# A running sum over sorted edges: chunks of 2048 in place of steps of 1024, and the mask as bytes by a broadcasting transfer

## Chip, core and metric

One Trainium2 chip, one of its cores. The metric is the device time of one execution in microseconds (us). TensorE is called PE, VectorE DVE, ScalarE ACT, GpSimd POOL and SyncE SP, as in the profile. SP issues nearly all plain transfers, POOL the indirect ones.

## What is computed

Two graph layers on 12,500 nodes of 64 channels and 212,500 edges, which come sorted by their target `dst`. Cut to what matters here (the second layer):

```python
h = relu(layernorm(x))
e = concatenate([h[src], edge_attr], axis=1)        # 212500 x 128
e = e @ W1a + b1a                                   # 212500 x 128
e = relu(batchnorm(e) * g1a + be1a)                 # statistics over all edges
# ( @ W2a + b2a ) and the sum over the edges of a node change places in the kernel
s = segment_sum(e, dst, 12500)                      # 12500 x 128
x = x + mlp(concatenate([h, s @ W2a + degree * b2a]))
```

The first layer is an edge network too, with a maximum over the edges of a node in place of the sum.

## The kernel before

It runs six stages one after the other, each a block in which every engine has its own program and waits on semaphores. A barrier of all engines ends a stage.

1. Index work: where each node's edges begin and end in the sorted list, and a mask that is 1 where an edge has the same target as the edge before it. It lies in `m01` (104 rows of 2048 edges, bf16) and goes to DRAM as `same_sum`. SP fills `recv_edges` with 1 MB transfers (L348), POOL scatters into it.
2. The edge network of layer 1: POOL gathers rows of source nodes.
3. Maxima are collected per node, the layer norm follows.
4. The hidden layer of layer 2, in 416 blocks of 512 edges: POOL gathers, PE transposes and multiplies, `finish` (L1126) writes hidden values into `hid` and takes their statistics; SP's `store` (L994) writes two blocks at a time, 512 KB, to `hid_edges`, channels on partitions.
5. The running-sum stage (L1150 to L1257), which nearly the whole change is about.
6. Node sums are taken as differences, then the node network.

Stage 5 walks over 212,992 edges (padded) in 208 steps k of STEP = 1024 edges. Channels lie on the 128 partitions, edges along the free dimension. A running sum is restarted at each new target by multiplying it by the mask: total[e] = mask[e] * total[e-1] + relu(gain * hid[e] + shift). The sum at the last edge of a node is that node's sum. In a step:

- SP `load` (L1176) fetches 1024 columns of `hid_edges`, 4 KB for each partition, into one of U = 8 slots (free again after the relu), then the step's mask, 2 KB on one partition, into one of R = 4 slots.
- PE `spread` (L1207) multiplies a column of ones by the mask row, so that the mask stands on all partitions in PSUM (`ps_mask`).
- ACT `relu` (L1228) writes `act_out`, two slots; it waits for the scan of step k-2.
- DVE `running_sum` (L1248) scans: `total` from `ps_mask`, `act_out` and the last column of the previous step's `total`.
- PE `turn_back` (L1215) transposes the 1024 columns with eight 128x128 transposes, so that edges lie on partitions, into `ps_back`.
- ACT `rows_out` (L1234) copies them to `rows`, SP `store` (L1188) writes them back, 512 KB, over the space of `hid_edges` that the step has read.
- SP `confirm` (L1183) waits for a store to land and raises `steps_out`; POOL (L1195) gathers the last row of each node's edges, 128 nodes at a time (100 gathers), once `steps_out` has reached the number in `steps_needed`.

The order on an engine is written by `pipeline(eng, steps, unroll, stages)` (L78 and on): at turn i each stage of the list, in the order of the list, is run for step i minus its lag. So ACT runs relu(k), rows_out(k-1), relu(k+1), rows_out(k), and SP runs load(k), store(k-5), confirm(k-8).

Of the kernel before, what the change touches and what calls it, by code (L numbers as in the profile page):

```python
# [20 lines left out]
P = 128  # L21
# [6 lines left out]
I16 = mybir.dt.int16  # L28

# [49 lines left out]
def pipeline(eng, steps, unroll, stages):  # L79
# [9 lines left out]
    assert rounds * unroll == steps and rounds > first and last <= unroll  # L89
# [14 lines left out]
    for step in range(steps - unroll, steps + last):  # L104
        peeled(step)


def gnn_kernel(nc, x, src, dst, edge_attr, W1, b1, W2, b2, W1a, b1a, g1a, be1a, W2a, b2a,
# [7 lines left out]
    STEP = 2 * BLK  # L116
    CO = 2048
# [5 lines left out]
    STEP_BITS = STEP.bit_length() - 1  # L123
    assert STEP == 1 << STEP_BITS
# [23 lines left out]
    def dram(name, shape, dt=F32):  # L148
        return nc.dram_tensor(name, shape, dt, kind="Internal").ap()
# [3 lines left out]
    same_sum = dram("same_sum", (EP,), BF16)  # L153
# [5 lines left out]
    hid_edges = dram("hid_edges", (NBLK // 2, P, 2 * BLK))  # L159
# [4 lines left out]
    with stack:  # L164
# [25 lines left out]
        steps_needed = tensor(stack, "steps_needed", [1, NI], I32)  # L190
# [51 lines left out]
        with ExitStack() as s1:  # L242
# [5 lines left out]
            mbig = tensor(s1, "mbig", [NCO, CO], BF16)  # L248
            firsts = tensor(s1, "firsts", [NCO, CO // GRP])
# [71 lines left out]
            def _(sp):  # L321
# [32 lines left out]
                sp.wait_ge(masks_made, 2)  # L354
                sp.dma_start(same_sum.rearrange("(p c) -> p c", c=CO), m01[:, :]).then_inc(masks_out, 16)
# [168 lines left out]
            def _(dve):  # L524
# [73 lines left out]
                nc.vector.tensor_scalar(mbig[:, :], m01[:, :], 2 * BIG, -BIG, ALU.mult, ALU.add).then_inc(masks_made, 1)  # L598

# [39 lines left out]
                once.link(nc.vector.tensor_scalar(column_end_i[:, :], column_end_i[:, :], STEP_BITS, None, ALU.logical_shift_right))  # L639
                once.link(nc.vector.tensor_scalar(steps_needed[:, :], column_end_i[:, :], 1, None, ALU.add))  # L640
# [290 lines left out]
        with ExitStack() as s4:  # L931
# [6 lines left out]
            hid = tensor(s4, "hid", [P, U // 2, 2, BLK])  # L938
# [22 lines left out]
            stored = [sem(f"stored4_{i}") for i in range(U // 2)]  # L961
# [7 lines left out]
            def _(sp):  # L969
# [24 lines left out]
                def store(r, s):  # L994
                    if s % 2 == 0:
                        return
                    at_least(sp, hid_made, r * U + s + 1)
                    sp.dma_start(hid_v[:, bass.ds(r * (U // 2) + s // 2, 1), :].rearrange("p a f -> p (a f)"),
                                 hid[:, s // 2, :, :].rearrange("p b q -> p (b q)")).then_inc(stored[s // 2], 16)

                pipeline(sp, NBLK, U, [(0, load), (5, store)])
                for q in range(U // 2):
                    sp.wait_ge(stored[q], 16 * (NBLK // U))
# [121 lines left out]
            def _(dve):  # L1125
                def finish(r, s):  # L1126
                    k = r * U + s
                    at_least(dve, multiplied, k + 1)
                    at_least(dve, stored[s // 2], 16 * r)
                    part = hid[:, s // 2, s % 2, :]  # L1130
# [19 lines left out]
        with ExitStack() as s5:  # L1150
            U = 8
            R = 4
            JS = STEP // P
            STEPS = EP // STEP
            hid = tensor(s5, "hid5", [P, U, STEP])
            mask_in = tensor(s5, "mask_in5", [1, R, STEP], BF16)
            ones5 = tensor(s5, "ones5", [1, P], BF16)
            act_out = tensor(s5, "act_out", [P, 2, STEP])
            total = tensor(s5, "total", [P, 2, STEP])
            rows = tensor(s5, "rows5", [P, R, JS * HID])  # L1160
            ps_mask = [banks(s5, f"ps_mask5_{b}", [P, STEP]) for b in range(2)]
            ps_back = [banks(s5, f"ps_back5_{b}", [P, JS * HID]) for b in range(2)]
            loaded = [sem(f"loaded5_{i}") for i in range(U)]
            stored = [sem(f"stored5_{i}") for i in range(R)]
            begun, mask_spread, relu_done, sum_done, back_turned, rows_made = (
                sem(n + "5") for n in ("begun", "mask_spread", "relu_done", "sum_done", "back_turned", "rows_made"))
            steps_out, sums_got, pool_passed = sem("steps_out"), sem("sums_got"), sem("pool_passed5")
# [274 lines left out]
```

## Time and profile before

| | us |
|---|---|
| median of 3 runs | 6878.51 |
| lowest and highest | 6867.25, 6896.64 |
| span of the profiled execution, first to last instruction | 5487.3 |
| median less span | 1391.2 |
| PE busy | 2916.4 (53%) |
| DVE busy | 2048.7 (37%) |
| ACT busy | 1440.8 (26%) |
| POOL busy | 3571.2 (65%) |

The profile holds one execution. Its own time beyond the span isn't recorded; what a timed run has besides the span is taken from the median. Times in the trace count from the span's start. Busy time counts work on data, not waits, branches or the issuing of transfers. The page cuts the span in 40 slices of 137 us and shows the busy share of an engine in tenths; the row PEclk has the granted TensorE clock in tenths of 2.4 GHz. Where an engine stood idle, the trace names what ended the idle time ("releaser").

### The profile page before, as it was taken

What the parts mean: (1) busy time and instruction counts of PE and PEld (TensorE: products, weight loads), DVE (VectorE), ACT (ScalarE), POOL (GpSimd) and SP (SyncE); (2) the same over time, 40 slices, a digit from 0 to 9 for tenths busy, and PEclk for the clock granted to TensorE, in tenths of its full rate; (3) what the DMA queues carried; (4) which work ended last, traced back from release to release, by engine and by line L of the source; (5) the groups of instructions that cost most, each with busy time, mean ns of one, the idle gap of its engine ahead of it and who ended that gap; (6) DMA issues with size and microseconds to landing.
All of it is one profiled execution on the core that took longest, in us unless ns stands there. A gap on an engine that the chain in (4) does not pass through costs nothing. (4 is left out here: it accounts for less than half of the span.)

```text
span 5487.3 us, 47739 instructions
## 1 busy us (share of the span) xinstructions
PE 2916.4 (53%) x8675; PEld 1611.3 (29%) x8675; DVE 2048.7 (37%) x2739; ACT 1440.8 (26%) x2694; POOL 3571.2 (65%) x3776
## 2 busy tenths in 40 slices
PE   2035555555555555521555555555555554888887
PEld 2023222332332233210222222222222222455455
DVE  7123333333333333344222222222222223666774
ACT  8011111111111111111222222222222221666663
POOL 6677777777777777766777777777777776111112
PEclk9975555556555655555666666666666666555556
DMA  9623233233233322322333333333333333899992
GB/s 353 207 62 78 78 80 80 77 79 80 78 78 80 80 76 80 80 53 64 105 103 106 107 101 106 107 104 103 107 105 103 107 107 89 311 322 321 321 322 70
DMA packets 396210, 695.12 MB, mean 127 GB/s; under 512 B 138632, under 2 KB 195730, under 8 KB 389410
## 3 DMA queue, kind: packets, MB, share of 16 engines
q1 hardware_dynamic: 250135, 558.29, 29.3%
q0 software_dynamic: 119328, 128.91, 12.4%
q10 hardware_dynamic: 26706, 7.50, 0.6%
q14 instruction: 31, 0.25, 0.0%
q8 instruction: 10, 0.16, 0.0%
HBM read 349.70 MB, written 344.74 MB: 127 GB/s over the span
## 5 line engine op out<-in xcount | busy, mean ns | idle before, releaser
L1014 POOL DMA_INDIRECT pairs<-norm_table,send_idx x1664 | 1573.9, 946 | 526.1 <-issue 506.8
L729 POOL DMA_INDIRECT send_in<-send_table,send_idx x1664 | 1574.3, 946 | 507.7 <-issue 505.1
L1028 PE MATMUL ps_pairs<-ident,pairs 128*128 128x128 f32 x1664 | 400.3, 387 | 991.1 <-issue 744.3
L1131 DVE TENSOR_SCALAR hid<-ps_hid,vec 128x512 f32<-128x512 f32 x416 | 312.2, 751 | 1384.0 <-PE ps_hid L1035 1384.0
L1035 PE MATMUL ps_hid<-pairs_t,w1a 128*128 128x512 f32 x832 | 711.2, 953 | 0.0
L1028 PEld LDWEIGHTS ps_pairs<-ident,pairs 128*128 128x128 f32 x1664 | 262.2, 195 | 1438.9 <-issue 1279.9
L1070 ACT COPY pairs_t<-ps_pairs 128x512 f32<-128x512 f32 x416 | 244.0, 586 | 1473.6 <-PE ps_pairs L1028 1473.6
L741 PE MATMUL ps_msg<-hidden,w_twice 128*128 128x512 f32 x416 | 431.1, 1140 | 307.9 <-ACT hidden L794 307.9
L763 PE MATMUL ps_send<-ident,send_in 128*128 128x128 f32 x832 | 216.3, 410 | 689.7 <-DMA send_in<-send_table,send_idx 689.7
L1254 DVE TENSOR_TENSOR_SCAN total<-ps_mask,total,act_out 128x1024 f32<-128x1024 f32 x208 | 488.8, 2350 | 215.3 <-ACT act_out L1232 215.1
L1201 POOL DMA_INDIRECT node_sums<-hid_edges,end_idx x100 | 94.6, 946 | 643.4 <-SPq L1186 636.9
L810 DVE TENSOR_TENSOR_SCAN maxima<-mask,maxima,ps_msg 128x512 f32<-128x512 f32 x208 | 266.2, 1280 | 600.3 <-PE ps_msg L741 600.3
L1220 PE MATMUL ps_back<-ident,total 128*128 128x128 f32 x1664 | 410.3, 427 | 98.1 <-DVE total L1254 98.1
L1220 PEld LDWEIGHTS ps_back<-ident,total 128*128 128x128 f32 x1664 | 327.2, 221 | 278.9 <-DVE total L1254 259.6
L819 DVE TENSOR_TENSOR_SCAN filled<-mask,filled,ps_recv 128x512 f32<-128x512 f32 x208 | 266.2, 1280 | 322.9 <-ACT mask L782 322.9
L763 PEld LDWEIGHTS ps_send<-ident,send_in 128*128 128x128 f32 x832 | 137.9, 203 | 781.4 <-DMA send_in<-send_table,send_idx 781.4
L782 ACT COPY mask<-ps_mask 128x512 f32<-128x512 f32 x208 | 121.9, 586 | 898.1 <-PE ps_mask L759 898.1
L794 ACT ACTIVATE hidden<-joined 128x512 f32<-128x512 f32 x208 | 130.9, 629 | 827.3 <-DVE joined L827 827.3
L827 DVE TENSOR_TENSOR joined<-filled,ps_send 128x512 f32<-128x512 f32 x208 | 143.1, 688 | 493.1 <-PE ps_send L763 493.1
L1134 DVE BATCH_NORM_STATS2 stats<-hid 128x512 f32 (+1 forms) x416 | 288.3, 693 | 98.1 <-DVE hid L1131 97.5
L756 PE MATMUL ps_recv<-ident,recv_in 128*128 128x128 f32 x832 | 210.8, 405 | 136.9 <-DMA mask_in<-same_max 136.9
L1238 ACT COPY rows<-ps_back 128x1024 f32<-128x1024 f32 x208 | 210.5, 1012 | 255.3 <-PE ps_back L1220 255.3
(176 smaller groups left out, 3184.6 us busy)
## 6 DMA issues: line engine op xcount, KB each, us to landing
hid_edges<-hid SPq DMA_DIRECT2D x208, 512.0 KB, 2.9
hid<-hid_edges SPq DMA_DIRECT2D x208, 512.0 KB
hid_edges<-rows SPq DMA_DIRECT2D x208, 512.0 KB, 3.8
recv_edges<-node_sums SPq DMA_DIRECT2D x52, 1024.0 KB
recv_in<-recv_edges SPq DMA_DIRECT2D x208, 256.0 KB
max_edges<-max_rows SPq DMA_DIRECT2D x208, 256.0 KB, 2.1
edge_in<-in_edge_attr_dram SPq DMA_DIRECT2D x415, 128.0 KB, 3.1
send_in<-send_table,send_idx POOLq DMA_INDIRECT x1664
```

Source lines behind the costliest of these rows:

```text
L729: pool.indirect_dma_start(out=send_in[:, s, j, t, :], out_offset=None, in_=send_table, in_offset=bass.IndirectOffsetOnAxis(ap=send_idx[:, ...
L741: nc.tensor.matmul(ps_msg[:, :], w2_twice[:, :], hidden[:, s % 2, :], start=True, stop=True).then_inc(msg_done, 1)
L763: mm = nc.tensor.transpose(ps_send[s % 2][:, j::J], send_in[:, s, j, :, :].rearrange("p t c -> p (t c)"), ident[:, :])
L810: nc.vector.tensor_tensor_scan(maxima[:, s % 2, :], mask[:, s % 2, :], ps_msg[:, :], maxima[:, 1 - s % 2, BLK - 1:BLK], ALU.min, ALU.max). ...
L819: nc.vector.tensor_tensor_scan(filled[:, s % 2, :], mask[:, s % 2, :], ps_recv[s % 2][:, :], filled[:, 1 - s % 2, BLK - 1:BLK], ALU.min, A ...
L1014: pool.indirect_dma_start(out=pairs[:, s, j, 0:C], out_offset=None, in_=norm_table, in_offset=bass.IndirectOffsetOnAxis(ap=send_idx[:, s / ...
L1028: mm = nc.tensor.transpose(ps_pairs[s % 2][:, j::J], pairs[:, s, j, :], ident[:, :])
L1035: nc.tensor.matmul(ps_hid[s % 2][:, :], w1a[:, :], pairs_t[:, s % 2, :], start=True, stop=True).then_inc(multiplied, 1)
L1131: nc.vector.tensor_scalar(part, ps_hid[s % 2][:, :], vec[:, 0:1], None, ALU.add).then_inc(hid_made, 1)
L1134: nc.vector.bn_stats(stats[:, bass.ds(k, 1), :].rearrange("p a q -> p (a q)"), part[:, 0:valid]).then_inc(stats_made, 1)
L1220: mm = nc.tensor.transpose(ps_back[s % 2][:, j * P:(j + 1) * P], total[:, s % 2, j::JS], ident[:, :])
L1254: nc.vector.tensor_tensor_scan(total[:, s % 2, :], ps_mask[s % 2][:, :], act_out[:, s % 2, :], total[:, 1 - s % 2, STEP - 1:STEP], ALU.mul ...
```

## The change

- Stage 5 goes over 104 chunks of 2048 edges, 1 MB and 8 KB per partition for each load and each store. Relu and scan work in two halves of 1024, transposes in two groups of eight; the relu is written in place over `hid` (four slots), so that a slot comes free after the scan.
- The mask of a chunk is fetched from DRAM by a transfer that repeats its 2048 bytes for all 128 partitions, into one of two slots; it is of type uint8. The mask product on PE and its PSUM tiles are gone; all eight PSUM banks serve `ps_back`.
- The orders are new: SP runs store(k-5), load_mask(k-3), load(k), confirm(k-8); ACT relu and rows_out of the chunk before last, in halves by turns.
- Stage 4 stores four blocks (1 MB) at a time. Stage 1 makes a copy of the mask in bytes. `pipeline` takes a number of steps that the unrolling doesn't divide.

```diff
-    for step in range(steps - unroll, steps + last):
+    for step in range((rounds - 1) * unroll, steps + last):
...
-                sp.wait_ge(masks_made, 2)
-                sp.dma_start(same_sum.rearrange("(p c) -> p c", c=CO), m01[:, :]).then_inc(masks_out, 16)
+                sp.wait_ge(masks_made, 3)
+                sp.dma_start(same_sum.rearrange("(p c) -> p c", c=CO), m01_bytes[:, :]).then_inc(masks_out, 16)
...
+                nc.vector.tensor_copy(m01_bytes[:, :], m01[:, :]).then_inc(masks_made, 1)
...
-                    if s % 2 == 0:
+                    if s % 4 != 3:
                         return
                     at_least(sp, hid_made, r * U + s + 1)
...
             @block.sync
                 def load(r, s):
                     k = r * U + s
-                    at_least(sp, relu_done, k - U + 1)
-                    sp.dma_start(hid[:, s, :], hid_v[:, bass.ds(k, 1), :].rearrange("p a f -> p (a f)")).then_inc(loaded[s], 16)
-                    at_least(sp, mask_spread, k - R + 1)
-                    sp.dma_start(mask_in[:, s % R, :], mask_v[:, bass.ds(k, 1), :].rearrange("t a c -> t (a c)")).then_inc(loaded[s], 16)
+                    at_least(sp, sum_done, 2 * (k - HR + 1))
+                    sp.dma_start(hid[:, s % HR, :], hid_v[:, bass.ds(k, 1), :].rearrange("p a f -> p (a f)")).then_inc(loaded[s % HR], 16)
+
+                def load_mask(r, s):
+                    k = r * U + s
+                    at_least_apart(sp, sum_done, 2 * (k - 1), sp_passed)
+                    sp.dma_start(masks[:, s % 2, :], mask_v[bass.ds(k, 1), :].rearrange("k c -> (k c)").partition_broadcast(P)).then_inc(masks_in[s % 2], 16)
...
                 def store(r, s):
                     k = r * U + s
-                    at_least(sp, rows_made, k + 1)
+                    at_least(sp, rows_made, 2 * (k + 1))
...
-                pipeline(sp, STEPS, U, [(0, load), (5, store), (U, confirm)])
+                pipeline(sp, CHUNKS, U, [(5, store), (3, load_mask), (0, load), (8, confirm)])
...
             @block.tensor
+                def turn_back(r, s, h):
+                    k = r * U + s
+                    if h == 0:
+                        at_least(pe, sum_done, 2 * (k + 1))
+                    at_least(pe, rows_made, 2 * k + h - 3)
+                    for j in range(JS // 2):
+                        mm = nc.tensor.transpose(ps_back[s % 2 * 2 + h][:, j * P:(j + 1) * P], total[:, s % 2, h * (JS // 2) + j::JS], ident[:, :])
+                    mm.then_inc(back_turned, 1)
...
             @block.scalar
+                def relu(r, s, h):
+                    if h == 0:
+                        at_least(act, loaded[s % HR], 16 * (r * (U // HR) + s // HR + 1))
+                    part = hid[:, s % HR, h * HALF:(h + 1) * HALF]
+                    nc.scalar.activation(part, part, ACT.Relu, bias=shift[:, 0:1], scale=gain[:, 0:1]).then_inc(relu_done, 1)
+
+                def rows_out(r, s, h):
+                    k = r * U + s
+                    at_least(act, back_turned, 2 * k + h + 1)
+                    if h == 0:
+                        at_least(act, stored[s % R], 16 * (r * (U // R) + s // R))
+                    nc.scalar.copy(rows[:, s % R, h * HALF:(h + 1) * HALF], ps_back[s % 2 * 2 + h][:, :]).then_inc(rows_made, 1)
+
+                pipeline(act, CHUNKS, U, [(0, lambda r, s: relu(r, s, 0)), (2, lambda r, s: rows_out(r, s, 0)),
+                                          (0, lambda r, s: relu(r, s, 1)), (2, lambda r, s: rows_out(r, s, 1))])
...
             @block.vector
+                def running_sum(r, s, h):
+                    k = r * U + s
+                    if h == 0:
+                        at_least(dve, masks_in[s % 2], 16 * (r * (U // 2) + s // 2 + 1))
+                    at_least(dve, relu_done, 2 * k + h + 1)
+                    if h == 0:
+                        at_least(dve, back_turned, 2 * (k - 1))
+                    at_least(dve, sum_done, 2 * k + h)
+                    before = total[:, 1 - s % 2, CHUNK - 1:CHUNK] if h == 0 else total[:, s % 2, HALF - 1:HALF]
+                    part = slice(h * HALF, (h + 1) * HALF)
+                    nc.vector.tensor_tensor_scan(total[:, s % 2, part], masks[:, s % 2, part], hid[:, s % HR, part],
+                                                 before, ALU.mult, ALU.add).then_inc(sum_done, 1)
```

## Rows read from the trace of the kernel before

**Rows 1.** The page, 40 slices of the span: PE, its clock, DMA.
```profile
PE   2035555555555555521555555555555554888887
PEclk9975555556555655555666666666666666555556
DMA  9623233233233322322333333333333333899992
```

**Rows 2.** Table by stretches, stage 5: length, busy us of each engine, clock, DMA share, GB/s.
```profile
4700.00:5360.00 660.00, 568.55 (x1961) 332.96 (x1960) 460.78 (x197) 421.63 (x394) 88.00 (x93) 0.50 0.93 321
```

**Rows 3.** Groups, 4700 to 5360 us: line, out<-in, shapes, count, busy us, mean ns, idle before.
```profile
L1254 DVE TENSOR_TENSOR_SCAN total<-ps_mask,total,act_out 128x1024 f32<-128x1024 f32 x197 | 462.9, 2350 | 200.8 <-ACT act_out L1232 200.8
L1220 PE MATMUL ps_back<-ident,total 128*128 128x128 f32 x1568 | 386.6, 427 | 91.4 <-DVE total L1254 91.4
L1212 PE MATMUL ps_mask<-mask_in,ones 1*128 1x512 bf16 x393 | 202.5, 616 | 0.0
```

**Rows 4.** Waits, 4700 to 5360 us: who waited for whom, us, times, longest.
```profile
DVE total L1254 <- ACT act_out L1232: 200.8, 197, 1.7
```

**Rows 5.** Timeline from 4998 us: start, duration, engine, line, operation, idle before it.
```profile
4997.76 2.35 DVE L1254 TENSOR_TENSOR_SCAN total<-ps_mask,total,act_out 128x1024 f32<-128x1024 f32 x1 [0.44 <-ACT act_out L1232]
...
5000.24 1.97 PE L1220 MATMUL ps_back<-ident,total 128*128 128x128 f32 x8
...
5002.24 1.01 ACT L1238 COPY rows<-ps_back 128x1024 f32<-128x1024 f32 x1 [0.63 <-PE ps_back L1220]
5003.15 1.24 ACT L1232 ACTIVATE act_out<-hid,shift,gain 128x1024 f32<-128x1024 f32 x1
5003.28 0.35 SPq L1191 DMA_DIRECT2D hid_edges<-rows  x1
...
5004.48 2.35 DVE L1254 TENSOR_TENSOR_SCAN total<-ps_mask,total,act_out 128x1024 f32<-128x1024 f32 x1 [0.43 <-ACT act_out L1232]
```

**Rows 6.** SP's queue: packets, MB, engine share; 4700-5360, 4668-4671, 30-60 us.
```profile
q1 hardware_dynamic: 56839, 205.92, 90.1%
q1 hardware_dynamic: 270, 0.97, 90.2%
q1 hardware_dynamic: 1548, 10.61, 84.4%
```

**Rows 7.** Tile hid_edges, 4700 to 5360 us: the stores of 512 KB, issue to landing.
```profile
DMA to landing us min/median/max: 2.9/3.9/4.9
```

**Rows 8.** Tile hid_edges, 2600 to 4500 us (stage 4): the same.
```profile
DMA to landing us min/median/max: 2.7/2.9/3.1
```

**Rows 9.** Timeline, the start of stage 5.
```profile
4666.00 0.34 SPq L1179 DMA_DIRECT2D hid<-hid_edges  x1
...
4666.40 0.28 SPq L1181 DMA_DIRECT2D mask_in<-same_sum  x1
...
4670.50 2.49 ACT L1232 ACTIVATE act_out<-hid,shift,gain 128x1024 f32<-128x1024 f32 x2 [6.46 <-DMA mask_in<-same_sum]
...
4671.88 4.84 DVE L1254 TENSOR_TENSOR_SCAN total<-ps_mask,total,act_out 128x1024 f32<-128x1024 f32 x2 [5.58 <-ACT act_out L1232]
```

**Rows 10.** Timeline, the end of stage 5: last scan, last gather.
```profile
5367.97 2.35 DVE L1254 TENSOR_TENSOR_SCAN total<-ps_mask,total,act_out 128x1024 f32<-128x1024 f32 x1 [0.52 <-ACT act_out L1232]
...
5379.33 0.94 POOL L1201 DMA_INDIRECT node_sums<-hid_edges,end_idx  x1 [0.30 <-issue]
```

**Rows 11.** Timeline, the end of stage 4: SP's last two stores, and bn_aggr.
```profile
4641.09 11.15 SPq L998 DMA_DIRECT2D hid_edges<-hid  x2
...
4652.13 11.42 DVE L232 BATCH_NORM_AGGREGATE sums<-stats 128x2 f32<-128x2496 f32 x1
```

**Rows 12.** Stage 1: DVE's mask instruction (timeline), POOL's wait for the fills.
```profile
158.49 0.68 DVE L598 TENSOR_SCALAR mbig<-m 104x2048 bf16<-104x2048 bf16 x1
...
POOL recv_edges L406 <- SPq L347: 16.0, 2, 15.7
```

More of the change, by code:

```diff
@@ L88, in pipeline @@
     first = 2 if last else 1
-    assert rounds * unroll == steps and rounds > first and last <= unroll
+    assert rounds > first and last <= unroll
     def peeled(step):
@@ L116, in gnn_kernel @@
     STEP = 2 * BLK
+    CHUNK_BITS = (4 * BLK).bit_length() - 1
+    assert 4 * BLK == 1 << CHUNK_BITS
     CO = 2048
@@ L960, in gnn_kernel @@
             gathered = [sem(f"gathered4_{i}") for i in range(U)]
-            stored = [sem(f"stored4_{i}") for i in range(U // 2)]
+            stored = [sem(f"stored4_{i}") for i in range(U // 4)]
             idx_copied, w_in, turned, copied, multiplied, hid_made, stats_made, root_ready, root_made = (
@@ L1128, in finish @@
                     at_least(dve, multiplied, k + 1)
-                    at_least(dve, stored[s // 2], 16 * r)
-                    part = hid[:, s // 2, s % 2, :]
+                    at_least(dve, stored[s // 4], 16 * r)
+                    part = hid[:, s // 4, s % 4, :]
                     nc.vector.tensor_scalar(part, ps_hid[s % 2][:, :], vec[:, 0:1], None, ALU.add).then_inc(hid_made, 1)
@@ L1221, in turn_back @@
                     mm.then_inc(back_turned, 1)
-                pe.wait_ge(begun, 2)
-                pipeline(pe, STEPS, U, [(0, spread), (1, turn_back)])
+                pipeline(pe, CHUNKS, U, [(0, lambda r, s: turn_back(r, s, 0)), (0, lambda r, s: turn_back(r, s, 1))])
             @block.scalar
             def _(act):
-                def relu(r, s):
-                    k = r * U + s
-                    at_least(act, loaded[s], 32 * (r + 1))
-                    at_least(act, sum_done, k - 1)
-                    nc.scalar.activation(act_out[:, s % 2, :], hid[:, s, :], ACT.Relu, bias=shift[:, 0:1], scale=gain[:, 0:1]).then_inc(relu_done, 1)
@@ L1234, in rows_out @@
-                def rows_out(r, s):
-                    k = r * U + s
-                    at_least(act, back_turned, k + 1)
-                    at_least(act, stored[s % R], 16 * (r * (U // R) + s // R))
-                    nc.scalar.copy(rows[:, s % R, :], ps_back[s % 2][:, :]).then_inc(rows_made, 1)
-                pipeline(act, STEPS, U, [(0, relu), (1, rows_out)])
+                def relu(r, s, h):
[3 more added lines that the diff above has]
+                    nc.scalar.activation(part, part, ACT.Relu, bias=shift[:, 0:1], scale=gain[:, 0:1]).then_inc(relu_done, 1)
```

88 lines of the change are left out of this document (35 added, 53 removed).

## The prediction

> **What bounds the kernel now.** I read the page first, then one table by stretches, then the groups, the waits and a timeline of the running-sum stage (the fifth stage), because nearly every edit is in it. The page's DMA row is at 9 in the slices of this stage (the 35th to the 39th) and at 2 or 3 in the long gather stages before it, and the clock row falls to 5 [rows 1]. PE's own row stands at 5 in those gather stages, with the clock at 5 or 6. So the first suspicion is that the stage is bound by transfers. The stretch 4700 to 5360 us confirms DMA 93% busy at 321 GB/s, but also PE 569 of 660 us at a granted clock of 0.50, the 1.2 GHz level [rows 2]. In the groups no engine is full: DVE's scan takes 2350 ns x 197 and still idles 200.8 us, the transposes make 386.6 us and the mask product 202.5 us of PE's time [rows 3]. What ends DVE's idle time is always ACT's relu, never a DMA [rows 4].
>
> The timeline shows why. From the end of a scan (4997.76 + 2.35 = 5000.11): transposes 5000.24 to 5002.21, copy 5002.24 to 5003.25, relu to 5004.39, next scan of the same parity 5004.48 [rows 5]. ACT does relu(k+1) only behind rows_out(k-1), which waits for the transposes of sum k-1. That loop takes 6.72 us for two steps of 1024 edges. Its links follow each other without a gap, so the stage is bound by a handshake of engines, with DMA close behind. In 2048-edge units the period is 6.7 us, and I compare all that follows with it.
>
> **The change, part by part.** Write T for the time of a 2048-edge chunk afterwards, s(m) for the end of its second half scan.
>
> Removed: the mask product (197 of 2x512 columns in the stretch, 202.5 us of PE) and the order relu behind rows_out of the previous step. Relu now needs only its load. So the old loop is gone. Engine work per chunk: DVE 2 x 2.35 plus a handshake, about 4.9 us; ACT two relus of 1.24 and two copies of 1.01, 4.5; PE 16 transposes, 3.8 at 1.2 GHz [rows 5]. None of these reaches 6.7.
>
> DMA per chunk: 1.05 MB in, 1.05 MB out, and new 262 KB for the mask written to 128 partitions, where 4 KB went before. Rates, each divided by the queue's share of the engines: 346 GB/s in this stage (205.92 MB, 660 us, 90.1%), 358 at its start where only loads run (0.97 MB, 3 us), 419 for the 1 MB fills of 8 KB per partition (10.61 MB, 30 us, 84.4%) [rows 6]. No row has loads with 8 KB rows. So 1 MB out takes 2.5 us, 1 MB in 2.5 to 2.9, the mask 0.6 (by the fill's rate) to 1.0 (small rows; no transfer of 128 rows from one 2 KB source appears), the gathers 0.2. Sum 5.8 to 6.8 with a middle of 6.2: by DMA alone the stage would be between 13% shorter and unchanged.
>
> Added: a wait that decides, in SP's order. In a step SP does store(m-2), load_mask(m), load(m+3). store(m-2) waits for both row halves of chunk m-2, and the mask DMA sits behind that wait and then, on the same queue, behind the 1 MB just issued. Yet sum m cannot start without that mask. This is a new loop over two chunks:
> - from s(m-2) to the store's issue: 0.13 + transposes 1.97 + 0.04 + copy 1.01 + relu of the second half 1.24 + copy 1.01, less two overlaps of 0.1, is 5.2 us [rows 5]. The second eight transposes end by 3.9 and are hidden by copy and relu.
> - from the store's issue to the mask's landing: a 512 KB store lands 3.9 us after issue in this stage [rows 7] and 2.9 in the uncrowded stage before [rows 8]. With 1.25 us of that being bytes (at 419 GB/s), 1.65 is fixed. A 1 MB store: 1.65 + 2.5 = 4.15; the mask behind it adds 0.6 to 1.0: 4.9. Upper end: with the 1.0 us of crowding that 3.9 shows, and bytes at 346 GB/s, 6.5. Lower end 4.5. I take 5.5.
> - the two half scans: two scans in a row took 4.84 us at the start of the stage [rows 9], with the handshake to the mask 4.9. A scan with both operands in SBUF and byte masks has no row; I take the PSUM one, with -0.2 to +0.3 us each as bounds.
> The sum is 15.6. PE is busy half the time instead of 86%; the gather stages with that share show a clock of 5 or 6 [rows 1], so a part of the transposes may run at 2.4 GHz, where 1.97 becomes 1.0: less 0.2. That makes 15.4 for two chunks, T = 7.7 us against 6.7. DMA then has 1.5 us of slack per chunk and engines more: the loop sets the pace.
>
> That a transfer does wait behind the one ahead of it is shown at the stage's start: load at 4666.00, its 2 KB mask issued at 4666.40, and relu starts at 4670.50 although relu needs both only; loading 512 KB at 358 GB/s is 1.5 us and the rest is latency and queueing [rows 9]. On order, the Trainium skill ("DMA: Bandwidth & Descriptors", Queues, rings and completion order) says that each DMA engine consumes descriptors of a ring in order, though a later one may finish first; this agrees with the start of the stage, and speaks for the loop. The same page (Rules for kernel authors) asks for 128 partitions and at least 1 MiB per DMA for the highest bandwidth; here the 1 MB fills do move more per busy time than the 512 KB transfers, so by that rule the stage would take the DMA sum's 6.2 instead of 7.7, which is the rival B1 below.
>
> Start: mask(0) is issued behind three 1 MB loads. The 4.5 us that the first 512 KB took, 2.5 MB more at 2.7 us, and 0.8 for the mask are 12.0 us to landing, so s(0) = 17.0 and s(1) = 21.8 (today the first scan starts after 5.9 us). Then 51 pairs: s(103) = 21.8 + 102 T = 807.2. Today the last scan ends 704.3 us after the stage's first load (5367.97 + 2.35 - 4666.00 [rows 9, 10]). Tail: today the last gather starts 9.0 us after the last scan. After: 4.9 to the last store, 4.2 to its landing, then four gathers that need chunk 103 at 1.25 apart: 13.1. Difference: 807.2 + 13.1 - 704.3 - 9.0 = 102 T - 678.4 = +107 us.
>
> Edits at nothing: the hidden-layer stage stores 1 MB every four blocks instead of 512 KB every two. It is paced by POOL's gathers, the same hid slots come free at least four blocks (20 us) ahead, and the last store, issued about 4652, lands around 4656 while bn_aggr alone runs 11.42 us from 4652.13 [rows 11]; without that cover it would cost 1.3 us. The mask copy to bytes in the first stage is one DVE instruction of about the 684 ns of its neighbour, at most 2; POOL's scatters, behind it, wait up to 15.7 us for the fills anyway [rows 12]. The semaphore rename and shift cost nothing.
>
> The profile gives 5487.3 us of span, the timed runs 6878.5; the 1391 us outside the span I take as constant. If they scaled with the span, +107 would be +134. Sum: 6878.5 + 107 = 6985.5, about 6985.
>
> **The rivals.**
> A (forecast): the mask loop, T from 7.2 to 8.3: +56 to +168.
> B1: the mask does not queue behind the store (or only its tail). Then the loop is 5.2 + 0.6 + 2.3 + 4.8 = 12.9, under 6.5 a chunk, and DMA sets 6.2 to 6.4: -46 to -26 us, say 6840. For it: fills at 419 GB/s. Against it: the stage start, and that all these transfers go through one queue.
> B2: the same with loads no faster than 358 and a mask of 1.0 us: T 6.6 to 6.9, -5 to +25, about 6888.
> C: slower still. 128 reads of the same 2 KB are not priced by bytes. From 1 us more on for the mask the loop reaches 16.6, T 8.3 and more, +168 to +230: 7046 to 7109. Nothing in the profile shows such a read; only its place in the loop speaks for it.
> D: the clock returns to 2.4 GHz for most of the stage: pair 14.6, T 7.3, +66. It stays inside A.
>
> **How the numbers follow.** A with D 0.66, B1 0.12, B2 0.12, C 0.10. A time within 0.5% (34 us) is about what a measurement can't tell from no change. B1 lies on that edge and beyond with part of it; A's lower end spills a little into "same". Faster 0.11, same 0.15, slower 0.74. The range leaves out most of B1 and the far end of C: 6885 to 7080, the likeliest case A holding 6934 to 7047.
>
> **What would show it.** Right: in the timeline of the stage DVE's first half scan waits 2 us or more for the mask's DMA, every time; the store is issued about 5.2 us behind s(m-2) and the mask's landing 5 to 6 us later; DMA share falls from 93% to about 80 to 88%; chunks are 7.7 apart. Wrong: DMA still at 93% or more with chunks under 6.7 apart (B1, B2), or the mask's landing over 7 us behind the store's issue (C). A first scan earlier than 9 us into the stage would refute the start's term, a wait for hid slots in the stage before the zero there.

## Result and profile after

| | before | after |
|---|---|---|
| median, us | 6877.78 (4 runs) | 7075.07 (4 runs) |
| lowest to highest | 6867.25 to 6896.64 | 7069.56 to 7079.55 |
| ratio, 95% interval | | 1.0283, 1.0266 to 1.0299 |

The changed kernel is slower by 197 us. The prediction said 6985 with a range of 6885 to 7080: the direction and the mechanism hold, the size does not. +107 was forecast, so the cost was taken at a little over half. 7075 is above the 7047 at which the likeliest case of the prediction ended. It lies in the range, by 5 us, only because the range's upper end had been drawn for rival C, whose cause is not the one found below. That much is luck.

One thing has to be said of the numbers first. The profiled execution of before spans 5487 us, and I took the 1391 us up to its timed runs for work outside the span. That is wrong. The trace of after spans 7068.9 us at a time of 7071, and a second trace of before 5473.9 at a time of 5476. The kernels ran on several chips. On one kind a stall comes at nearly every turn of the loops in the gather stages, on the other there is none. Before takes about 6880 us on the first kind (chip 13; for the first result no chip is noted) and 5477 on the second (chips 4, 9 and 10). That it is the chip, and not something else of the occasion, is likely but not shown. The difference between the two kernels is nearly the same on both kinds, and a chunk of after takes 8.58 and 8.61 us on them (below); before has been traced on the second kind only. So stage 5 can be read from any of these traces, and each ratio is taken to runs of before on the same chip. A difference in us between two changed kernels goes by way of before.

The page of after, answering to [rows 1]:

```profile
PE   1033333333333333331233333333333333333336
PEclk9975555555666555565565656565666566656666
DMA  9312221111221121221222222222222222677783
```

The slices are longer (177 us), and in stage 5, from the 35th on, DMA stands at 6 to 8 where it stood at 9. In numbers, for a stretch of stage 5 (answering to [rows 2]), then SP's queue in the same stretch ([rows 6]):

```profile
6200.00:6800.00 600.00, 232.01 (x1104) 208.74 (x1104) 327.03 (x140) 288.30 (x276) 113.67 (x65) 0.61 0.78 278
```

```profile
q1 hardware_dynamic: 29785, 162.58, 75.7%
```

DMA is busy 78% and moves 278 GB/s, against 93% and 321. PE is busy 39%, DVE 55%, ACT 48%: nothing is full. What DVE waits for, in the groups and the waits ([rows 3, 4]):

```profile
L1258 DVE TENSOR_TENSOR_SCAN total<-masks,total,hid 128x1024 f32<-128x1024 uint8 x140 | 329.1, 2351 | 279.8 <-DMA masks<-same_sum 272.5
L1220 PE MATMUL ps_back<-ident,total 128*128 128x128 f32 x1104 | 232.0, 396 | 371.9 <-DVE total L1258 371.9
```

```profile
DVE total L1258 <- DMA masks<-same_sum: 272.5, 70, 7.5
```

The scan's time is unchanged at 2351 ns, with bytes in SBUF as its mask. 272.5 of its 279.8 idle us end with the landing of a mask. The timeline of two chunks shows the loop (answering to [rows 5]; start, duration, engine, line):

```profile
6479.00 4.80 DVE L1258 TENSOR_TENSOR_SCAN total<-masks,total,hid 128x1024 f32<-128x1024 uint8 x2 [7.04 <-DMA masks<-same_sum]
...
6483.93 3.33 PE L1220 MATMUL ps_back<-ident,total 128*128 128x128 f32 x16 [8.98 <-DVE total L1258]
6483.98 0.33 SPq L1184 DMA_DIRECT2D hid<-hid_edges  x1
6484.62 4.81 DVE L1258 TENSOR_TENSOR_SCAN total<-masks,total,hid 128x1024 f32<-128x1024 uint8 x2 [0.82 <-DMA masks<-same_sum]
...
6486.02 1.01 ACT L1238 COPY rows<-ps_back 128x1024 f32<-128x1024 f32 x1 [8.54 <-PE ps_back L1220]
6486.93 1.24 ACT L1231 ACTIVATE hid<-hid,shift,gain 128x1024 f32<-128x1024 f32 x1
6488.07 1.00 ACT L1238 COPY rows<-ps_back 128x1024 f32<-128x1024 f32 x1
...
6489.10 0.36 SPq L1198 DMA_DIRECT2D hid_edges<-rows  x1
...
6489.70 0.33 SPq L1189 DMA_DIRECT2D masks<-same_sum  x1
6490.30 0.94 SPq L1184 DMA_DIRECT2D hid<-hid_edges  x1
...
6494.21 0.36 SPq L1198 DMA_DIRECT2D hid_edges<-rows  x1
6494.81 0.48 SPq L1189 DMA_DIRECT2D masks<-same_sum  x1
6496.16 4.81 DVE L1258 TENSOR_TENSOR_SCAN total<-masks,total,hid 128x1024 f32<-128x1024 uint8 x2 [6.73 <-DMA masks<-same_sum]
```

Scans end at 6483.80. Transposes, copy, relu and copy follow, and the store is issued at 6489.10, 5.30 us later. The mask is issued at 6489.70, and the scans that need it begin at 6496.16. The loop is 17.16 us for two chunks, 8.58 each. The chunks between, of the other parity, run the same loop with a lag of 5.6 us rather than half the period. So DVE's waits come by turns: 7.04 us at one chunk, 0.82 at the next. Over chunks 12 to 91 of this trace the means are: 5.1 us from the end of a sum to its store's issue, 7.5 from there to the scan that needs the mask (6.4 to 9.3), 4.8 for the two half scans.

Start and end of stage 5 (answering to [rows 9, 10]):

```profile
6050.18 2.42 SPq L1184 DMA_DIRECT2D hid<-hid_edges  x3
...
6052.64 0.44 SPq L1189 DMA_DIRECT2D masks<-same_sum  x1
...
6062.07 9.75 DVE L1258 TENSOR_TENSOR_SCAN total<-masks,total,hid 128x1024 f32<-128x1024 uint8 x4 [11.76 <-DMA masks<-same_sum]
```

```profile
6945.35 4.81 DVE L1258 TENSOR_TENSOR_SCAN total<-masks,total,hid 128x1024 f32<-128x1024 uint8 x2 [1.44 <-DMA masks<-same_sum]
```

```profile
6962.85 0.95 POOL L1208 DMA_INDIRECT node_sums<-hid_edges,end_idx  x1 [0.30 <-issue]
```

From the first load to the last gather's start the stage takes 912.7 us, and took 713.3 [rows 9, 10]. The 199 us between them are the whole difference of the kernels.

### The profile page after: what moved, and what is told of

The parts are those of the page before. It is cut to its first block and busy times, and to the rows that moved or that the text cites. A ratio compares the mean times of both kernels' runs of the same rounds, so it can differ in the third digit from the quotient of the medians.

```text
span 7068.9 us, 44176 instructions
## 1 busy us (share of the span) xinstructions
PE 2417.4 (34%) x8259; PEld 1492.4 (21%) x8259; DVE 2039.6 (29%) x2739; ACT 1421.3 (20%) x2694; POOL 3637.2 (51%) x3776
## 5 line engine op out<-in xcount | busy, mean ns | idle before, releaser
L1040 PE MATMUL ps_hid<-pairs_t,w1a 128*128 128x512 f32 x832 | 623.8, 842 | 1000.4 <-ACT pairs_t L1075 572.1
L1258 DVE TENSOR_TENSOR_SCAN total<-masks,total,hid 128x1024 f32<-128x1024 uint8 x208 | 489.0, 2351 | 410.9 <-DMA masks<-same_sum 399.9
L1033 PE MATMUL ps_pairs<-ident,pairs 128*128 128x128 f32 x1664 | 334.4, 337 | 692.4 <-ACT pairs L1081 493.6
L1208 POOL DMA_INDIRECT node_sums<-hid_edges,end_idx x100 | 163.6, 1636 | 773.7 <-SPq L1193 767.4
L1220 PE MATMUL ps_back<-ident,total 128*128 128x128 f32 x1664 | 346.2, 393 | 572.1 <-DVE total L1258 572.1
L746 PEld LDWEIGHTS ps_msg<-hidden,w_twice 128*128 128x128 f32 x416 | 99.7, 298 | 1906.4 <-ACT hidden L799 1522.9
L1220 PEld LDWEIGHTS ps_back<-ident,total 128*128 128x128 f32 x1664 | 310.2, 218 | 607.8 <-issue 324.3
L1040 PEld LDWEIGHTS ps_hid<-pairs_t,w1a 128*128 128x128 f32 x832 | 170.0, 254 | 1055.0 <-ACT pairs_t L1075 589.6
L1231 ACT ACTIVATE hid<-hid,shift,gain 128x1024 f32<-128x1024 f32 x208 | 258.6, 1244 | 7.5 <-DMA hid<-hid_edges 7.4
```

Source lines behind the costliest of these rows:

```text
L746: nc.tensor.matmul(ps_msg[:, :], w2_twice[:, :], hidden[:, s % 2, :], start=True, stop=True).then_inc(msg_done, 1)
L1033: mm = nc.tensor.transpose(ps_pairs[s % 2][:, j::J], pairs[:, s, j, :], ident[:, :])
L1040: nc.tensor.matmul(ps_hid[s % 2][:, :], w1a[:, :], pairs_t[:, s % 2, :], start=True, stop=True).then_inc(multiplied, 1)
L1220: mm = nc.tensor.transpose(ps_back[s % 2 * 2 + h][:, j * P:(j + 1) * P], total[:, s % 2, h * (JS // 2) + j::JS], ident[:, :])
L1231: nc.scalar.activation(part, part, ACT.Relu, bias=shift[:, 0:1], scale=gain[:, 0:1]).then_inc(relu_done, 1)
L1258: nc.vector.tensor_tensor_scan(total[:, s % 2, part], masks[:, s % 2, part], hid[:, s % HR, part], before, ALU.mult, ALU.add).then_inc(sum ...
```

## Experiments

"A chunk takes" means below: the time from the first half scan to the last (both in the row of the scan, the number after "x208" being the least, median and largest duration), less 2.4 us, over 103. By that after has 8.58 us and before 6.73 for 2048 edges.

**The two kernels on the other kind of chip.** `before_again` and `after_again` are the kernels unchanged.

> The kernel before, unchanged, for a second trace of it. The profiled execution of before spans 5487 us while its timed runs take 6878; the one of the changed kernel spans 7069 and its runs take 7075. If the 1391 us are stalls that one trace of before happened not to have, this trace spans about 6870, its gather stages (2 and 4) have a stall at each turn of their loops of 14 and 11 us, and its running-sum stage takes the same 714 us as in the first trace. If the 1391 us lie outside the span, it spans about 5487 again. If the running-sum stage has stalls of its own, it is longer than 714 here and the comparison by stage has to be made again.

> The changed kernel itself, unchanged, beside the kernel before on the chip of the experiments, where before takes 5477 us and not 6878. If the difference of the two kernels comes from the running-sum stage alone, it is +190 to +205 us here too (5667 to 5682), and the stage shows chunks 8.6 us apart. If the stalls of the loops on the first chip took part in the difference, it is smaller here, +107 or less.

Measured: before 5475.67 with a span of 5473.9, after 5678.17, ratio 1.0368 (1.0351 to 1.0386), so +202 here against +197. The line of POOL's waits for ACT in stage 2, of after (first kind of chip), then of before_again:

```profile
POOL send_in L734 <- ACT send_idx L781: 781.5, 54, 16.3
```

```profile
POOL send_in L729 <- ACT send_idx L776: 3.6, 11, 0.5
```

54 waits of about 14 us in a loop of 52 turns of four steps; the same wait comes to 3.6 us in all on the other kind, at most 0.5 at a time. What ACT stalls on at the turn no trace names. The queue that the profile calls q14 instruction moved 12 packets in stages 2 to 4 of after and 11 in those of before_again, so more fetching of code does not show. Loads and scans of stage 5, before_again, then after_again, with after_again's masks from issue to landing:

```profile
L1179 SPq DMA_DIRECT2D hid<-hid_edges x208: 327/333/1779, 4653.3 to 5341.6; - x104
```

```profile
L1184 SPq DMA_DIRECT2D hid<-hid_edges x104: 327/345/1043, 4655.5 to 5529.3; - x104
L1258 DVE TENSOR_TENSOR_SCAN total<-masks,total,hid x208: 2349/2350/2353, 4668.5 to 5557.9; 128x1024 f32<-128x1024 uint8 x104
...
DMA to landing us min/median/max: 5.0/7.0/11.8
```

Stage 5 begins 2.2 us later in after, so the 1 MB stores of stage 4 and the mask copy cost that much at most. A chunk takes 8.61 us. The mask lands 7.0 us (median) after its issue.

**The mask ahead of the store.**

```diff
-pipeline(sp, CHUNKS, U, [(5, store), (3, load_mask), (0, load), (8, confirm)])
+pipeline(sp, CHUNKS, U, [(3, load_mask), (5, store), (0, load), (8, confirm)])
```

> The changed kernel with one swap: SP issues the mask of chunk m ahead of the store of chunk m-2, not behind it. Theory (the loop through rows, store and mask sets the pace): the mask no longer waits for the rows copy nor for the 1 MB of the store; the loop of two chunks falls from 17.2 to about 12 us, so that transfers set the pace, 6.7 to 7.2 us a chunk in place of 8.6, and the time falls by 140 to 190 us to 6885 to 6935. Rival (what costs is the mask's transfer itself, its bytes or its reads of one source, wherever it stands in the queue): the chunk stays at 8.3 us or more and the time above 7040. Rival (loads and stores of 8 KB rows are slower): the same, above 7040.

Measured: 5452.0, ratio to before 0.9953 (0.9936 to 0.9970). That is 25 us under before where after is 202 over, so 227 less than after. The scan row, a table by stretches and one loop of the timeline:

```profile
L1258 DVE TENSOR_TENSOR_SCAN total<-masks,total,hid x208: 2349/2350/2404, 4667.4 to 5329.4; 128x1024 f32<-128x1024 uint8 x104
```

```profile
4800.00:5300.00 500.00, 268.23 (x1248) 241.29 (x1248) 366.14 (x157) 325.62 (x311) 113.50 (x73) 0.62 0.99 377
```

```profile
4897.97 4.80 DVE L1258 TENSOR_TENSOR_SCAN total<-masks,total,hid 128x1024 f32<-128x1024 uint8 x2 [2.11 <-PE ps_back L1220]
...
4902.95 0.34 SPq L1184 DMA_DIRECT2D hid<-hid_edges  x1
4903.62 0.74 SPq L1189 DMA_DIRECT2D masks<-same_sum  x1
...
4910.36 4.80 DVE L1258 TENSOR_TENSOR_SCAN total<-masks,total,hid 128x1024 f32<-128x1024 uint8 x2 [1.74 <-DMA masks<-same_sum]
```

The same transfers, with two entries of a list changed round, take 6.40 us a chunk, and now DMA is busy 99% at 377 GB/s. The loop was the bound, not the bytes. The gain is larger than expected (140 to 190), because a chunk of transfers takes 6.4 and not 6.7 to 7.2.

The timeline says what the swap took away. The mask is now issued 0.85 us after the sum two chunks back (4902.77 to 4903.62), where in after it came 5.9 us behind it. But it does not land sooner after its issue: 6.74 us here, behind a 1 MB load issued just before it, against 6.46 behind a 1 MB store. What costs is SP's wait for the rows, in front of the mask, more than the store's bytes. (Five kernels are set side by side below.)

**No mask traffic.** Only the first two masks are fetched, and the scans no longer wait for one.

```diff
 def load_mask(r, s):
     k = r * U + s
-    at_least_apart(sp, sum_done, 2 * (k - 1), sp_passed)
+    if not (isinstance(k, int) and k < 2):
+        return
```

> The changed kernel without the mask's traffic: only the masks of the first two chunks are fetched, and all later chunks use these two, so its sums are not those of the reference. It prices the 8 KB transfers alone. Theory: 2.1 MB a chunk at 2.5 us out and 2.7 in make 5.2 to 5.6 us a chunk, 104 of them 310 us less than 8.6 a chunk: 6740 to 6790. If loads and stores of 8 KB rows bring nothing over 4 KB rows, a chunk takes 6.2 or more and the time is above 6810. If the wait for the mask was not the bound, it stays above 7000.

Measured: 5317.7, ratio 0.9708 (0.9691 to 0.9724).

```profile
L1259 DVE TENSOR_TENSOR_SCAN total<-masks,total,hid x208: 2349/2351/2406, 4666.9 to 5195.6; 128x1024 f32<-128x1024 uint8 x104
```

```profile
4700.00:5100.00 400.00, 231.80 (x1249) 209.52 (x1250) 368.16 (x157) 323.67 (x311) 84.97 (x74) 0.75 1.01 419
```

A chunk takes 5.11 us at 419 GB/s (the expectation, put on the other chip's 7075, is about -310; measured -360 against 5678). DVE, busy 92%, waits for ACT, and ACT for loads, so transfers set the pace. The 8 KB loads and stores by turns reach the 419 GB/s of the fills alone. The mask costs 6.40 - 5.11 = 1.29 us of DMA time, twice the 0.63 of its 262 KB at this rate (1.20 by the 6.31 of the kernel with three mask slots, below).

**Is it the one source row?** As the kernel with the mask ahead, but each mask transfer reads 128 different rows of 2048 bytes of `same_sum`, which aren't the chunk's mask.

```diff
-mask_v[bass.ds(k, 1), :].rearrange("k c -> (k c)").partition_broadcast(P)
+mask_v
```

> The kernel with the mask ahead of the store (5452 us, 6.41 us a chunk, DMA 99% busy), but each mask transfer reads 128 different rows of 2 KB, always the same region, in place of one row 128 times; the masks are those of all chunks at once, so its sums are not those of the reference. Without the mask's traffic a chunk takes 5.13 us, so the mask costs 1.28, and by bytes at 419 GB/s it should cost 0.63. Theory (many reads of one 2 KB source are slow): 5.75 to 5.9 us a chunk, 50 to 70 us less, 5382 to 5402. Rival (2 KB rows cost this much whatever their source): 5440 to 5460, no change.

Measured: 5451.16, ratio 0.9952 (0.9935 to 0.9969); a chunk takes 6.46.

```profile
L1259 DVE TENSOR_TENSOR_SCAN total<-masks,total,hid x208: 2349/2350/2419, 4667.4 to 5334.8; 128x1024 f32<-128x1024 uint8 x104
```

No change: the theory falls. Reading one row 128 times costs nothing extra over reading 128 rows, always the same 256 KB. That a transfer of 128 rows of 2 KB, put between transfers of 8 KB rows, takes twice its bytes is measured; why is open, and no run varies the rows' length.

**A third mask slot, the store still ahead.** Slots 2 to R = 3, the wait for the sum three chunks back, and:

```diff
-pipeline(sp, CHUNKS, U, [(5, store), (3, load_mask), (0, load), (8, confirm)])
+pipeline(sp, CHUNKS, U, [(5, store), (2, load_mask), (0, load), (8, confirm)])
```

> The changed kernel with a third mask slot: the order in a turn of SP stays store, mask, load, and the mask still stands behind a 1 MB store in its queue, but it is issued one chunk earlier (behind the store of chunk m-3). Theory (the loop over two chunks, closed by two mask slots and the lag of 3): a loop over three chunks of 10.1 + 7.1 us leaves 5.8 a chunk, so the transfers' own 6.4 us set the pace: 5445 to 5460, as with the mask ahead of the store. Rival (a mask behind a store is late whatever its lead): above 5550.

Measured, on the first kind of chip: 6837.03 against 6884.81, ratio 0.9931 (0.9914 to 0.9947), 48 us less than before.

```profile
L1258 DVE TENSOR_TENSOR_SCAN total<-masks,total,hid x208: 2350/2351/2396, 6061.3 to 6713.5; 128x1024 f32<-128x1024 uint8 x104
```

A chunk takes 6.31 us, and DMA is busy 100% at 381 GB/s. A mask behind a store does no harm once it is asked for one chunk earlier. So the loop over two chunks is shown from two sides, by order and by depth. Four slots, each mask issued ahead of its load, do not fit: `rows` needs 24,576 bytes of a partition and 24,032 are left, so the fully relaxed case has no time.

**The mask on another queue.** First issued by ACT behind its last copy:

```diff
-pipeline(sp, CHUNKS, U, [(5, store), (3, load_mask), (0, load), (8, confirm)])
+pipeline(sp, CHUNKS, U, [(5, store), (0, load), (8, confirm)])
...
-                          (0, lambda r, s: relu(r, s, 1)), (2, lambda r, s: rows_out(r, s, 1))])
+                          (0, lambda r, s: relu(r, s, 1)), (2, lambda r, s: rows_out(r, s, 1)), (0, load_mask)])
```

> The changed kernel with the mask's transfer issued by ACT behind its last rows copy, so at the same point of time as before, but on ACT's queue, not behind the store and load in SP's. Theory A (the mask waits for the 1 MB ahead of it in its queue): the mask lands 1.5 to 3 us earlier, a chunk takes 7.2 to 7.9 us, and the time is 75 to 145 us under that of the changed kernel. Theory B (the engines of DMA are shared whatever the queue, and only the late issue counts): a chunk stays at 8.3 us or more, within 35 us of the changed kernel.

Measured: 5489.49, ratio 1.0018 (1.0009 to 1.0028); 189 us less than after. Its ten times spread from 5475 to 5505, and a chunk takes 6.89 in the profiled one, which is the longest. The expectation's "same point of time" was wrong. ACT hands out the transfer while its copy still runs:

```profile
5003.25 0.34 ACTq L1232 DMA_DIRECT2D masks<-same_sum  x1
...
5004.62 0.35 SPq L1192 DMA_DIRECT2D hid_edges<-rows  x1
```

The mask is 1.4 us ahead of the store, where in after it is 0.6 behind. So queue and time were mixed, and a second kernel makes ACT wait for the copies (`rows_made` in place of `sum_done` in the wait before the transfer):

> As the kernel with the mask on ACT's queue (5489 us), but the mask's issue waits until the rows of the chunk before last are copied, which is what SP's store waits for. So mask and store are issued within 1 us of each other, as in the changed kernel (5678 us), and only the queue differs: the mask is no longer behind the 1 MB of the store. In the kernel with ACT's queue the mask was issued 1.9 us earlier than that. Theory A (standing behind the store in one queue is what counts): landing stays near 4.3 us, the loop of two chunks is 1.9 us longer than 13.8, so 7.8 us a chunk, 5575 to 5600. Theory B (only the time of issue counts; engines of DMA are shared): landing near 6.9 us as in the changed kernel, 8.4 us a chunk or more, 5650 and above. In both, a part of the 189 us between the two kernels is put down to the earlier issue.

Measured, on the first kind of chip: 7026.73 against 6884.81, ratio 1.0206 (1.0189 to 1.0223), +142; a chunk takes 8.11.

```profile
6203.19 0.34 SPq L1192 DMA_DIRECT2D hid_edges<-rows  x1
6203.20 0.37 ACTq L1232 DMA_DIRECT2D masks<-same_sum  x1
...
6210.60 4.80 DVE L1259 TENSOR_TENSOR_SCAN total<-masks,total,hid 128x1024 f32<-128x1024 uint8 x2 [2.05 <-DMA masks<-same_sum]
```

On its own queue, issued with the store, the mask shown here is ready 7.40 us later. That is one of the long ones: over chunks 12 to 91 it takes 3.9 to 7.9 us from issue to scan and 6.4 on average, against 6.9 in after. Two chunks are 0.9 us shorter than in after, half of it by the earlier issue and half by the landing. The time lies between the theories: +142 over before, where A gives +99 to +124 and B +174 or more. The landing is near B's. So another queue brings 0.9 us per two chunks, where the issue 1.4 us ahead of the store on the same queue brought 3.4.

**More in front of the mask.**

```diff
+sp.dma_start(extra[:, s % 2, :], mask_v[bass.ds(k, 1), 0:1760].rearrange("k c -> (k c)").partition_broadcast(P)).then_inc(masks_in[s % 2], 16)
 sp.dma_start(masks[:, s % 2, :], mask_v[bass.ds(k, 1), :] ...
```

> The changed kernel with a second broadcasting transfer of the mask, 1760 of the 2048 bytes for 128 partitions, into a tile that nothing uses, issued right ahead of each mask. By the runs so far a mask's transfer takes 1.28 us of DMA time, so this takes 1.1. Theory (the mask's landing is on a loop over two chunks, and everything that stands ahead of it in the queue is on it once): a chunk is 0.55 to 0.8 us longer, +56 to +82 us over the changed kernel, so +258 to +284 over the kernel before. By bytes alone (0.54 us, half a chunk's share) it would be +28 over the changed kernel. Rival (the slack of DMA, busy for 78%, takes it up): within 15 us of the changed kernel.

Measured: 5757.77, ratio 1.0510 (1.0492 to 1.0527): +281 over before, +79 over after.

```profile
L1260 DVE TENSOR_TENSOR_SCAN total<-masks,total,hid x208: 2349/2351/2353, 4669.2 to 5639.6; 128x1024 f32<-128x1024 uint8 x104
```

A chunk takes 9.40 us, 0.79 more, with DMA busy 87%: idle DMA doesn't take it up. Two chunks are 1.58 longer for an estimated 1.1 of DMA time in each (1.29 x 1760/2048). The mask is issued 0.4 us later behind the store, since SP has the other transfer to issue first, and its own landing is 0.9 us longer; how the rest comes about is not shown.

**The loop of the orders side by side.** Means over chunks 12 to 91 of each trace, us: from the end of the sum of chunk m-2 to the issue of mask m, from there to the start of scan m, and the two half scans.

| | sum to mask's issue | issue to scan | scans | two chunks |
|---|---|---|---|---|
| after_again: the changed kernel | 5.65 | 6.97 | 4.81 | 17.4 |
| mask_and_extra: more in front | 6.26 | 7.83 | 4.80 | 18.9 |
| mask_actq_late: ACT's queue, with the store | 5.22 | 6.43 | 4.81 | 16.5 |
| mask_actq: ACT's queue, ahead of the store | 3.82 | 5.32 | 4.81 | 13.9 |
| mask_first: SP's queue, ahead of the store's wait | 0.84 | 7.25 | 4.81 | 12.9 |

The first column is what the kernels mostly differ in. In mask_first, where DMA is busy 99%, this loop and the transfers' own time come out alike; a third slot, which opens the loop, brings only 0.09 us a chunk more, so there the transfers are the bound.

**What bounded the stage before.** The kernel before, one number changed:

```diff
-pipeline(act, STEPS, U, [(0, relu), (1, rows_out)])
+pipeline(act, STEPS, U, [(0, relu), (2, rows_out)])
```

> The kernel before with one number changed: ACT copies rows out two steps behind the relu, not one, so that relu(k+1) no longer waits for the transposes of sum k-1. Steps of 1024, 4 KB rows and the mask product stay. Theory (the stage was bound by that loop of engines, 3.36 us a step, with transfers 93% busy): transfers at 4 KB rows become the bound at 3.05 to 3.15 us a step, 45 to 65 us less, 5412 to 5432. Rival (transfers were the bound all the time): no change, 5470 to 5480. Rival (PE's 2.85 us a step and a new handshake): between, or slower than before.

Measured, on the first kind of chip: 6775.66 against 6884.81, ratio 0.9834 (0.9818 to 0.9851), 109 us less.

```profile
L1254 DVE TENSOR_TENSOR_SCAN total<-ps_mask,total,act_out x208: 2349/2349/2350, 6068.1 to 6661.2; 128x1024 f32<-128x1024 f32 x104
```

```profile
6100.00:6500.00 400.00, 400.00 (x1398) 237.29 (x1396) 328.06 (x140) 299.83 (x280) 62.46 (x66) 0.50 1.00 378
```

593.1 / 207 = 2.87 us a step in place of 3.36. The stage was bound by the loop of ACT, PE and DVE. The gain is twice what I expected, because 4 KB rows move 378 GB/s here; the 93% of before was no limit near at hand. Now PE is busy all the time at clock 0.50 (1.2 GHz) and DMA too. In this stretch DVE and ACT wait for PE, and no engine waits for a load, so PE looks like the bound, and 378 GB/s is no shown limit of 4 KB rows either.

**8 KB rows with the mask on PE.** Chunks of 2048 as in after; the mask arrives on one partition in halves, `ps_mask` and `ps_back` have two tiles each.

```diff
+def spread(r, s, h):
+    i, q = 2 * (r * U + s) + h, (2 * s + h) % R
+    at_least(pe, masks_in[q], 16 * (r * (2 * U // R) + (2 * s + h) // R + 1))
+    at_least(pe, sum_done, i - 1)
+    for a in range(0, HALF, BLK):
+        mm = nc.tensor.matmul(ps_mask[h][:, a:a + BLK], ones5[:, :], mask_in[:, q, a:a + BLK], start=True, stop=True)
+    mm.then_inc(mask_spread, 1)
...
+pipeline(sp, CHUNKS, U, [(2, lambda r, s: load_mask(r, s, 0)), (2, lambda r, s: load_mask(r, s, 1)),
+                         (5, store), (0, load), (8, confirm)])
```

> The part of the change with chunks of 2048 and 8 KB rows alone: the mask is spread by PE again as in the kernel before, from 2 KB on one partition, in halves of 1024; two PSUM tiles hold the mask and two the transposed sums. Transfers take 5.13 us a chunk (measured without mask traffic), DVE 4.9, PE 16 transposes and 4 mask products 5.7 at 1.2 GHz. Theory: PE sets 5.7 to 5.9 us a chunk in place of the 6.7 of before, so 75 to 105 us less than before, 5372 to 5402, the fastest so far. Rival (a handshake between PE, ACT and DVE closes a new loop because there are only two tiles each): 6.4 us a chunk or more, 5440 or more.

> The kernel with chunks of 2048, 8 KB rows and the mask product on PE once more, to stand beside the one-number change of the kernel before, which took 109 us off in another batch, where this kernel had taken 102 off. If PE at 1.2 GHz bounds both (5.70 and 5.73 us for 2048 edges), this one is again 95 to 115 us faster than before. If 8 KB rows bring something of their own, it is faster than by 120.

Measured: 5373.89, ratio 0.9813 (0.9797 to 0.9829), and again 5374.11, ratio 0.9815 (0.9798 to 0.9831): 103 us less than before.

```profile
L1269 DVE TENSOR_TENSOR_SCAN total<-ps_mask,total,hid x208: 2348/2350/2351, 4662.4 to 5252.4; 128x1024 f32<-128x1024 f32 x104
```

```profile
4700.00:5200.00 500.00, 394.28 (x1741) 275.91 (x1739) 408.79 (x174) 365.31 (x348) 77.02 (x82) 0.69 0.99 376
```

```profile
PE ps_mask L1229 <- DMA mask_in<-same_sum: 104.4, 66, 3.7
```

5.70 us a chunk as expected, but not by the reason given: PE is busy 79% at a clock of 0.69 and waits for its mask, while DMA is at 99%. DMA moves 376 GB/s here and 419 without mask traffic, so whether the transfers or a wait for the small masks sets this pace is not shown. It is the equal of the one-number change (109 and 103 us), with some 50 changed lines. Both beat both kernels of this study. The equality says little of 8 KB rows by themselves: the two kernels end at 5.73 and 5.70 us for 2048 edges with different engines waiting.

## Why the prediction was right in kind and short in size

- **Bound before**: the engines' loop, right, shown by the changed lag. Wrong was "with DMA close behind". I had divided the queue's bytes by its busy share of 90.1% to get 346 GB/s as what 4 KB rows can do; in all they did 378. The busy share is not in proportion to the rate (93% at 321 GB/s, 100% at 378), so it can't be scaled up to a limit; why it runs ahead is not shown.
- **DMA per chunk**: 5.8 to 6.8 with 6.2 in the middle; measured 6.40 (6.31 with three slots). Right in sum, wrong in parts: loads and stores 5.11 and not 5.2 to 5.6, the mask 1.2 to 1.3 and not 0.6 to 1.0.
- **The mask's loop**: right. s(m-2) to store 5.2, measured 5.30 (mean 5.1). Two scans 4.9, measured 4.81. The term that was mis-sized is the one from the store's issue to the mask's landing: 5.5 taken, 6.5 as its upper end, measured 7.06 (6489.10 to 6496.16; 7.65 for the other parity) and 7.5 on average. Its bytes were taken about 0.5 too low. The other 1.5 us is argued, not shown, to be crowding. The prediction had 1.0 us of crowding in its upper end only, and no term for the neighbours: a 1 MB load is issued 0.6 us behind the mask, and the other parity's store 4.5 us behind the mask. How the us divides is open.
- **What in front of the mask costs**: named as two things, the wait for the rows and the queue behind 1 MB. The first is shown: issued 4.8 us earlier by the swap, two chunks are 4.5 us shorter, with a landing no shorter. The second was taken as shown by the stage's start, where relu begins 4.1 us after the issue of a 2 KB mask. That row alone does not part queueing from latency. The kernel with ACT's late issue puts a bound on it: out of SP's queue, behind the same wait, the landing is 0.5 us shorter on average.
- **The sum**: 17.2 for 15.4, 0.9 us a chunk, some 90 us over the stage, is the whole miss (197 against 107). Start: the first scan 11.9 us in, where 12.0 was worked out. Tail: last scan to last gather 12.7, worked out 13.1 (its own terms give 12.9). Clock 0.61, as taken.
- **Signs**: store issue and DVE's wait for the mask came as said. The wait of 2 us or more "every time" did not: it is 7.04 and 0.82 us by turns. DMA share 78% lies just under 80 to 88, chunks 8.6 apart and not 7.7.
- **Edits at nothing**: 2.2 us at most. Right.
- **Outside the span**: wrong, told above. It did no harm, since the stalls are in both kernels.
- **Rivals**: B1 and B2 (mask not behind the store) fell: from the store's issue to the scan B1 had 2.9 us, measured 7.5. The time reached C's 7046 to 7109. Half of C is there: the mask's transfer is not priced by its bytes (about 1.25 us against 0.63). But reading one source is not why, since 128 reads of one 2 KB row cost no more than 128 rows, and the excess over the 0.6 to 1.0 taken is 0.2 to 0.7, less than the 1 us that C needs. My sign for C, a landing over 7 us behind the store's issue, therefore misleads: this kernel shows it without that much of C. D's clock stayed at 0.61.

Of the rules of the Trainium skill, the one on megabyte transfers, which the prediction weighed ("DMA: Bandwidth & Descriptors", Rules for kernel authors) agrees with 419 GB/s in the kernel without masks, but its gain is not to be had while a loop of waits is longer. The one on issuing engines, which it did not name (same page of the Trainium skill, Issuing engines are not separate DMA queues), that transfers of all of them run on the same engines and interleave, agrees with the mask on ACT's queue: issued in the same moment as the store it took 6.4 us to its scan on average; in SP's queue, 0.6 us behind the store, it took 6.9.

## What to carry to other kernels

Before transfers are made larger, close the question of what each is waiting for. A small transfer that an engine needs soon should not stand, in its issuer's program, behind a store that waits for the end of the pipeline; list for each transfer what is ahead of it, and add up the loop from sum to sum. Here the wait was the dear part, and a second queue behind the same wait helped little. When DMA is 93% busy and yet no engine ever waits for a load, look for a loop of handshakes first: a lag of 2 in place of 1 took off 109 us, where the whole change cost 197. And take a landing time from a row as crowded as the stage that you forecast: here even the upper end, 6.5 us, was passed by 1 us on average.

## What the runs showed of the hardware

- Gather loops that ran without a stall on chips 4, 9 and 10 (5477 us) had one of about 14 us at nearly every turn on another chip (6885 us), the kernel being the same; the cause is open. The profiled execution and the timed ones can be from either.
- 256 KB as 128 rows of 2 KB takes 1.2 to 1.3 us of DMA time between transfers of 8 KB rows, twice its bytes' share, whether the 128 rows are one or many in DRAM.
- Loads and stores of 8 KB rows in turn reach 419 GB/s; 4 KB rows with small masks reached 378 at least, while their busy share at 321 GB/s was already 93%.
- From issue to use, the 256 KB mask took 6.97 us right behind a 1 MB store (DMA busy 79%), 7.25 right behind a 1 MB load (99%), and 5.3 on another queue 1.4 us ahead of the store (94%).
- A scan takes the same 2350 ns for 1024 columns with a float mask in PSUM and with a byte mask in SBUF.
